# Cross-attention scores as one plain fp32 product instead of split fp32r products, an earlier closing order and all copies of turned probabilities on ScalarE, in a one-core decoder layer

## What is computed

```
x = layernorm(x + self_attention(x))                  # 32 heads of 16, alibi bias, causal
x = layernorm(x + cross_attention(x, ctx, ctx, mask)) # 32 query heads, 8 key/value heads, d 128, rope
x = layernorm(x + ffn(x))                             # relu^2 MLP 512-1024-512 + routed latent part, layernorm
```

## Time and profile before

| | |
|---|---|
| median of 3 runs | 913.37 us (911.8 to 914.2) |
| the profiled execution | 913.87 us, its span 911.5 us |
| busy: PE, DVE (VectorE), ACT (ScalarE), POOL (GpSimd) | 869.6, 654.2, 473.1, 556.1 us |
| mean granted TensorE clock | 0.988 of full speed |

### The profile page before, as it was taken

One profiled execution on the slowest core, in us unless ns is written; L12 is line 12 of the kernel. 1 busy time (PEld: TensorE's weight loads), 2 busy tenths in 40 slices (PEclk: granted clock), 3 DMA queues, 4 the chain that ended last, 5 costly groups with the idle time before them and its releaser, 6 DMA issues.

```text
span 911.5 us, 15714 instructions
## 1 busy us (share of the span) xinstructions
PE 869.6 (95%) x4780; PEld 721.2 (79%) x4780; DVE 654.2 (72%) x2171; ACT 473.1 (52%) x1509; POOL 556.1 (61%) x486
## 2 busy tenths in 40 slices
PE   7998899899999799999999999999999998999995
PEld 6787777687777588888888888888888887787884
DVE  5465688778877677777777777777777778546546
ACT  5335777877773355555555555555555556340310
POOL 4625866776677666666666666666666688463002
PEclk9999999999999999999999999999999999999998
DMA  8678999768768011311311313113122123000000
GB/s 284 242 222 190 222 205 177 164 164 171 162 202 300 26 36 38 130 39 36 128 36 45 118 36 127 36 36 128 36 78 85 36 70 105 12 24 24 24 12 35
DMA packets 68370, 96.64 MB, mean 106 GB/s; under 512 B 7232, under 2 KB 44352, under 8 KB 67264
## 3 DMA queue, kind: packets, MB, share of 16 engines
q1 hardware_dynamic: 68288, 95.65, 37.4%
HBM read 68.33 MB, written 27.26 MB: 105 GB/s over the span
## 4 chain that ended last, share of the span: by engine, by line
PE 79%; POOL 6%; DVE 5%; issue 4%; ACT 3%; DMA 1%; SPq 1%; POOLq 0%; ACTq 0%; DVEq 0%
PE banks L35 65%; PE banks L1135 4%; PE banks L1115 3%; PE banks L767 3%; PE banks L785 2%; PE banks L1136 2%; PE banks L758 1%; POOL x L1683 1%; POOL B_wv L171 1%; ACT C_prob L1056 1%; DMA heads_k<-heads_k_d 1%; POOL C_t L1271 1%; POOL B_prob L581 1%; PE banks L122 1%; SPq L213 1%
## 5 line engine op out<-in xcount | busy, mean ns | idle before, releaser
L35 PE MATMUL banks<-C_wo,C_o 128*128 128x512 f32 x768 | 191.8, 399 | 1.9 <-DVE C_o L1232 1.0
L35 PE MATMUL banks<-xT,C_w 128*128 128x512 f32 x768 | 186.6, 392 | 1.1 <-DVE xT L137 0.8
L35 PEld LDWEIGHTS banks<-xT,C_w 128*128 128x128 f32 x768 | 144.3, 189 | 31.9 <-issue 2.0
L35 PEld LDWEIGHTS banks<-C_wo,C_o 128*128 128x128 f32 x768 | 140.5, 190 | 30.6 <-issue 1.9
L1047 ACT ACTIVATE C_q<-C_t 128x512 fp32r<-128x512 f32 x64 | 40.5, 632 | 166.1 <-POOL C_t L1271 166.1
L688 ACT ACTIVATE B_prob<-B_prob,B_top 128x128 f32<-128x128 f32 x256 | 99.5, 391 | 40.1 <-DVE B_top L853 40.0
L1279 POOL TENSOR_TENSOR C_q<-C_t,C_q 128x512 fp32r<-128x512 f32 x64 | 82.8, 1294 | 46.0 <-ACT C_q L1047 46.0
L1056 ACT ACTIVATE C_prob<-C_prob,C_top 128x128 f32<-128x128 f32 x256 | 99.0, 391 | 0.0
L581 POOL TENSOR_TENSOR B_prob<-B_prob,B_rden 128x512 f32<-128x512 f32 x64 | 66.5, 1041 | 36.3 <-DVE B_rden L862 36.2
L1271 POOL TENSOR_TENSOR C_t<-C_t,C_t 128x512 f32<-128x512 f32 x64 | 82.8, 1294 | 6.2 <-DVE C_t L1189 5.9
L171 POOL TENSOR_TENSOR C_w<-stage,C_w 128x512 fp32r<-128x512 f32 x32 | 41.1, 1285 | 54.6 <-ACT C_w L166 54.5
(11 more groups left out here) (147 smaller groups left out, 1918.4 us busy)
## 6 DMA issues: line engine op xcount, KB each, us to landing
C_kv<-cross_kv_d SPq DMA_DIRECT2D x8, 2048.0 KB, 8.5
cross_kv_d<-B_k_out SPq DMA_DIRECT2D x16, 512.0 KB, 3.4
cross_kv_d<-B_v_out SPq DMA_DIRECT2D x16, 512.0 KB, 4.7
stage<-wq_dram SPq DMA_DIRECT2D x32, 256.0 KB, 2.6
stage<-wo_dram SPq DMA_DIRECT2D x32, 256.0 KB, 2.6
heads_q<-heads_q_d SPq DMA_DIRECT2D x96, 64.0 KB, 4.0
heads_k<-heads_k_d SPq DMA_DIRECT2D x96, 64.0 KB, 4.1
heads_q_d<-cT SPq DMA_DIRECT2D x8, 512.0 KB, 2.6
```

Of the source, the lines that this page charges most:

```text
L35: mm = eng.matmul(out, stationary[i], moving[j], start=first and n == 0, stop=last and n == len(PASSES) - 1)
```

## The change

- Cross scores: queries and keys are no longer split. `scores` is one plain fp32 matmul of 128 columns per head, into one bank per step, the two banks in turn; it waits for `minima(n-2)`. `key_hi`, `key_lo`, `tile_hi`, `tile_lo` and the subtraction at L1202 are gone; the GpSimd sums write keys and queries directly; the mask is negated once by ScalarE and read in the per-head minimum. A stored group of keys and values is 3/4 of the size.
- Self-attention: ScalarE copies all turned probabilities, VectorE none. `add_row`, `root` and `normalise` stand one step earlier (lags 15, 16, 17); `turn` stays at 19. The first four value weight pieces are split before step 0.
- End of stage A: context pieces are loaded and split earlier (split at tiles 16, 17, 18, 18, 19, 19, 20, 20 instead of 16 to 23).

```
-KV = 4 * NT
+KV = 3 * NT
...
+    LOAD_BEHIND = {7: (0,), 9: (1,), 11: (2,), 13: (3, 4), 15: (5, 6, 7)}
+    CONTEXT_AT = (16, 17, 18, 18, 19, 19, 20, 20)
...
-            [self.CONTEXT + i - self.QK] * (i >= self.QK)
+            [self.CONTEXT + k for k, tile in enumerate(self.CONTEXT_AT) if tile == i]
...
-            if i >= self.QK // 2 and i % 2 == 1:
-                self.load_piece(eng, self.CONTEXT + (i - self.QK // 2) // 2)
-        for n in range(self.CONTEXT + C, len(self.pieces)):
-            self.load_piece(eng, n)
+            for n in self.LOAD_BEHIND.get(i, ()):
+                self.load_piece(eng, self.CONTEXT + n)
...
-    PIECES = (("k", 0, -1), ("v", 0, 0), ("v", 1, 0), ("v", 2, 1), ("v", 3, 1), ("o", 0, 3), ("o", 1, 4), ("k", 1, 6),
+    PIECES = (("k", 0, -1), ("v", 0, -1), ("v", 1, -1), ("v", 2, -1), ("v", 3, -1), ("o", 0, 3), ("o", 1, 4), ("k", 1, 6),
...
-    OT, CLOSE, ROW, ROOT, NORMAL, TURN, TAKE = 13, (14, 15), 16, 17, 18, 19, 20
+    OT, CLOSE, ROW, ROOT, NORMAL, TURN, TAKE = 13, (14, 15), 15, 16, 17, 19, 20
...
-            eng.tensor_tensor(t1, t1, t2, ALU.add).then_inc(self.s_sum, 1)
+            eng.tensor_tensor(self.k_out[j % 2][:, :, :], by_batch(t1), by_batch(t2), ALU.add).then_inc(self.s_sum, 1)
...
-        if n >= self.LT and (n - self.LT) % 2 == 0:
+        if n >= self.LT:
             self.copy_turned(eng, n - self.LT)
...
         wait(eng, self.s_pv, (m - 4) // 2 + 1)
-        eng.activation(self.pT[:, m % 4, :], self.tp, ACT.Copy).then_inc(self.s_turned[0], 1)
+        eng.activation(self.pT[:, m % 4, :], self.tp, ACT.Copy).then_inc(self.s_turned, 1)
...
-        wait(eng, self.s_turned[(m - 1) % 2], (m + 1) // 2)
+        wait(eng, self.s_turned, m)
...
-        if n >= self.LT and (n - self.LT) % 2 == 1:
-            self.copy_odd(eng, n - self.LT)
...
     def scalar_end(self, eng):
 
-        self.key_hi(eng, len(self.FILL) // 2 - 1)
         self.value_hi(eng, len(self.FILL) // 2 - 1)
-        self.copy_turned(eng, self.NS - 2)
-        eng.wait_ge(self.s_klo, len(self.FILL) // 2)
+        for m in range(self.NS - 3, self.NS):
+            self.copy_turned(eng, m)
+        eng.wait_ge(self.s_sum, len(self.FILL) // 2)
...
+    def negate_mask(self, eng):
+
+        eng.wait_ge(self.s_mask, 16)
+        eng.activation(self.mask[:, :, :], self.mask[:, :, :], ACT.Copy, scale=-1.0).then_inc(self.s_negated, 1)
...
-            wait(eng, self.s_top, n)
+            wait(eng, self.s_top, n - 1)
             tok = slice(s % 4 * S, (s % 4 + 1) * S)
-            both = self.kv[g % 2][:, 2 * S * s:2 * S * (s + 1)]
+            keys = self.kv[g % 2][:, S * s:S * (s + 1)].bitcast(F32)
             for h in range(self.Q):
-                out = self.sc[:, h // 2, h % 2, :, :].rearrange("p j s -> p (j s)")
-                q = self.q[s // 4]
-                eng.matmul(out, q[0][:, h, tok], both, start=True, stop=False)
-                mm = eng.matmul(out[:, 0:S], q[1][:, h, tok], both[:, 0:S], start=False, stop=True)
+                mm = eng.matmul(self.sc[n % 2][:, h * S:(h + 1) * S], self.q[s // 4][:, h, tok], keys, start=True, stop=True)
...
-            for a in range(2):
-                added = eng.tensor_tensor(heads[:, a], self.sc[:, a, :, 1, :],
-                                          self.mask[:, n % B, :].unsqueeze(1).broadcast_to([P, 2, S]), ALU.subtract)
-            added.then_inc(self.s_masked, 1)
-            eng.wait_ge(self.s_masked, n + 1)
             eng.memset(self.carrier[:, :], 0.0)
             for h in range(self.Q):
                 last = eng.tensor_tensor_reduce(
-                    self.prob[:, n % 2, h * S:(h + 1) * S], self.sc[:, h // 2, h % 2, 0, :],
-                    self.prob[:, n % 2, h * S:(h + 1) * S], 1.0, 3.4e38, ALU.add, ALU.min,
-                    self.top[:, n % 2, h:h + 1])
+                    self.prob[:, n % 2, h * S:(h + 1) * S], self.sc[n % 2][:, h * S:(h + 1) * S],
+                    self.mask[:, n % B, :], 1.0, 3.4e38, ALU.add, ALU.min, self.top[:, n % 2, h:h + 1])
...
-        eng.tensor_tensor(t1, t1, t2, ALU.add).then_inc(self.s_sum, 1)
+        eng.tensor_tensor(self.query(r), by_batch(t1), by_batch(t2), ALU.add).then_inc(self.s_sum, 1)
```

More of the change, by code:

```diff
@@ L473, in __init__ @@
         self.v_out = pool("v_out", 88, [P, 2, HG, 2, P], F32R)
-        self.k_out = [pool(f"k_out{i}", (96, 132)[i], [P, 4, 2, S], F32R) for i in range(2)]
+        self.k_out = [pool(f"k_out{i}", (96, 132)[i], [P, 4, S]) for i in range(2)]
         self.bout = pool("bout", 126, [P, D])
@@ L622, in gpsimd_end @@
         self.rows.root(eng, B - 2)
-        self.key_lo(eng, len(self.FILL) // 2 - 1)
         for i in (3, 4):
@@ L693, in scalar @@
             self.value_hi(eng, j)
-        j = self.tile("k", n, 2)
-        if j is not None:
-            self.key_hi(eng, j)
         self.scalar_pieces(eng, n)
@@ L712, in scalar_end @@
             self.cross.piece_hi(eng, i)
-        self.cross.tile_hi(eng, 0)
         self.cross.piece_hi(eng, 7)
-        self.cross.tile_hi(eng, 1)
         self.rows.hi(eng, B - 1)
-        for r in (2, 3):
-            self.cross.tile_hi(eng, r)
     def project(self, eng, f, part):
@@ L773, in weigh @@
         b, c = k // C, k % C
-        for odd in range(2):
-            eng.wait_ge(self.s_turned[odd], k + 1)
+        eng.wait_ge(self.s_turned, 2 * k + 2)
         if k == 0:
@@ L910, in vector @@
             eng.wait_ge(self.s_pj, self.FILL.index(("k", j)) + 1)
-            wait(eng, self.s_klo, j - 1)
+            wait(eng, self.s_sum, j - 1)
             if j == 1:
@@ L968, in __init__ @@
         self.kv = [pool(f"kv{i}", (36, 16)[i], [P, KV], F32R) for i in range(2)]
-        self.q = [[pool(f"q{half}{lo}", 72 + 16 * half + 8 * lo, [P, self.Q, HALF], F32R) for lo in range(2)]
-                  for half in range(2)]
+        self.q = [pool(f"q{half}", 72 + 8 * half, [P, self.Q, HALF]) for half in range(2)]
         self.prob = pool("prob", 132, [P, 2, D])
@@ L992, in live, with query @@
         return 0 <= n - lag < self.NS
-    def query(self, r, lo):
-        return by_batch(self.q[r // self.Q % 2][lo][:, r % self.Q, :])
+    def query(self, r):
+        return by_batch(self.q[r // self.Q % 2][:, r % self.Q, :])
     def split(self, n):
@@ L1039, in piece_hi @@
         self.ring.hi(eng, self.first + i, self.target(i)[0])
-    def tile_hi(self, eng, r):
-        eng.wait_ge(self.s_sum, r + 1)
-        if r == self.Q:
-            for i in range(2):
-                eng.wait_ge(self.before.s_vout[i], 16 * B)
-        eng.activation(self.query(r, 0), by_batch(self.t1[:, r % 2, :]), ACT.Copy).then_inc(self.s_qhi, 1)
+    def negate_mask(self, eng):
+        eng.wait_ge(self.s_mask, 16)
+        eng.activation(self.mask[:, :, :], self.mask[:, :, :], ACT.Copy, scale=-1.0).then_inc(self.s_negated, 1)
     def exponentials(self, eng, n):
@@ L1068, in scalar @@
             self.next_piece_hi(eng, 1)
-        elif n + self.PRE < self.TILES:
-            self.tile_hi(eng, n + self.PRE)
         if self.live(n, 2):
@@ L1074, in scalar @@
             eng.activation(self.o[0][:, :], self.ov, ACT.Copy).then_inc(self.s_ohi, 1)
-        if n == 2:
-            self.tile_hi(eng, n + self.PRE)
+        if n == 0:
+            self.negate_mask(eng)
         if n != 1:
@@ L1185, in rotate @@
         eng.wait_ge(self.s_pj, r + 1)
-        wait(eng, self.s_qlo, r - 1)
+        wait(eng, self.s_sum, r - 1)
         eng.tensor_tensor(by_batch(t1), by_batch(bank), cos, ALU.mult).then_inc(self.s_cos, 1)
@@ L1370, in sync @@
             if n == self.DOWN:
-                eng.wait_ge(self.before.s_qlo, self.before.TILES)
+                eng.wait_ge(self.before.s_sum, self.before.TILES)
                 for t, name in ((self.gate, "gate"), (self.gamma, "gamma"), (self.beta, "beta")):
```

61 lines of the change are left out of this document (14 added, 47 removed).

## The result

| | before | after |
|---|---|---|
| median | 913.8 us (4 runs, 911.8 to 915.9) | 891.5 us (890.6, 892.4, 890.6) |
| the profiled execution, its span | 913.87, 911.5 us | 890.58, 888.6 us |
| mean granted TensorE clock | 0.988 | 0.995 |

The ratio is 0.975, 95% interval 0.972 to 0.978. A fourth execution of the changed kernel took 1744.7 us, for a reason that no trace shows, and is left out. Forecast was 891.0.

A forecast was written before the change was run, and what follows sets the result against it. PE bounds the long stretch of stage C; elsewhere waits set the time. From 913.87 us, terms of 0, -6, -7, -7 and -2.5 gave 891.4, forecast as 891; own range 884 to 898, widened to 883 to 903 for 8 in 10.

The forecast's parts named there:

- term 3: Steps 8 to 63 of stage B: waits before turns go, value projections come slightly later; -7 us, bounds -4 and -9.
- term 2: Stage A to step 8 of stage B: earlier loads and splits shorten idles and raise the clock; -6 us, bounds 3 and 8.
- terms 2 and 5: Start of stage B, -6 us from earlier loads and splits; last steps of C, -2.5 us from dropping L1202.
- Term 1: PE's cross scores: eight plain fp32 records cost the same 0.96 us a step as eight fp32r matmuls; 0 us.
- four passes against three: Cross scores: plain fp32 time scales with passes, +0.32 us a step, +20.5 in all, 911.5 us; chance 0.06.
- a load that isn't hidden: Cross scores: each plain fp32 record pays weight load plus stream, +0.88 us a step, 947 us; chance 0.05.
- these can now start when step 3's scores are done: Early stage B: SP's 12 head-data issues start earlier, against the 2.03 us hole for head data at 98.72.
- there is cover: Stage B: ScalarE's extra copies stay hidden, 2.5 us of ScalarE per step against 2.8 of PE.
- Term 4: From stage B to stage C: three idles shrink and the clock rises; -7 us, bounds 4 and 9.
- so the whole 0.75 is gained: Last steps of C: PE's own 5.2 us a step bounds next, so removing L1202 gains 0.75 us each time.
- The third rival: Stage B: ScalarE becomes the bound, copies late by 0.15 to 0.3 us in 56 steps; 898 to 906 us; chance 0.11.
- the fourth: Starts of B and C keep their holes as other waits take over, giving 5 instead of 13; 899 us; chance 0.13.

The follow-up runs named there:

- the doubled scores: The kernel before and the changed kernel, each with every cross score computed twice; 969.0 and 950.2 us.
- `piece_loads_late`: Changed kernel with SP loading each weight piece of stage B one step later; 889.2 us, ratio to before 0.973.
- `close_late`: Changed kernel with add_row, root and normalise back at lags 16, 17, 18; 891.5 us, ratio to before 0.978.
- `four_edits`: Changed kernel with later B piece loads, odd copies on VectorE, GpSimd's normalisation before its split early in C, ScalarE's D splits after its turned copy; 884.3 us.
- `gpsimd_relieved`: Changed kernel with four normalisations in the last steps of C moved from GpSimd to VectorE; span 890.7 us.
- `exps_ahead`: Changed kernel with ScalarE's exponentials ahead of its copy of the outputs in the last three steps of C; span 892.4 us.
- `both_relieved`: Changed kernel with, in C's last steps, ScalarE's exponentials ahead of its output copy and four normalisations moved from GpSimd to VectorE; span 893.5 us.

## Why the prediction was right

The forecast of 891.0 met 891.5. That it came out to half a microsecond is luck. By the borders that the prediction draws, the terms measured -1.3, -6.1, -6.1, -8.7 and -0.6 us against 0, -6, -7, -7 and -2.5, and the misses cancel. The second and third look better so than their reasons were: the moved hole at step 12 lies in the stretch of term 3 but comes from the reason given in term 2. Below I count it there, with the border at step 13, and then two terms that gave less than predicted (2 and 5) are made up by three that gave more. The five terms' bounds, simply added, would give 881 to 904 us; the range of 884 to 898 is narrower, and the prediction does not say how it was drawn from them.

- **Term 1 (0, measured -1.3).** Right, by the reason given. A record of 128 fp32 columns at full width costs 0.112 us, an fp32r matmul of the old scores 0.115, both about the pitch of weight loads. The distance to the outputs fell from 0.96 to 0.81 us, but the group before it grew by 0.08. The check named in the forecast, that distance alone, would have shown 0.15 us a step where 0.02 were gained. The rivals of four passes against three (+0.32 us a step) and of a load that isn't hidden (+0.88) are excluded by the doubled scores. The Trainium skill (FP8 and Floating Point Precision, TensorE Precision Notes) has four passes for fp32; no run here counts passes, and read as time against three fp32r products it would be wrong for this shape.
- **Term 2 (-6, measured -3.6).** Mis-sized. By step 8, where the term ended, the lead was 6.1 us (scores of step 8 at 92.61, near the 94 of the forecast) and by step 11 7.6. The step that failed is "these can now start when step 3's scores are done": true for the heads of step 8, but it did not ask what SP is late with next. That is one weight load waiting 3.0 us for GpSimd, ahead of the heads of step 12; hole and slow clock behind it took 4.0 us back, 2.5 and 1.5. `piece_loads_late` shows this by removing it.
- **Term 3 (-7, measured -8.7).** Size nearly right, attribution partly wrong. The turns lose their waits: the six steps that hold them are 8.8 us shorter, counted at 8.4. But the earlier lags add at most 0.6 us to this (`close_late`); what goes away on GpSimd and VectorE is enough for it, by the estimate above `key_lo` alone. The sum read `normalise` as 1.25 us long and did not ask why; it takes 0.52 where GpSimd has no 128x512 operation beside it. The price of ScalarE's extra copies, for which "there is cover", is 1.9 us, at the output projections; without it the term would have been -10.6. The lateness of `value_lo`, counted at 1.4 us, did not show.
- **Term 4 (-7, measured -8.7).** Within its bounds. Holes of 0.94, 2.65 and 2.32 us became one of 2.10, and the clock went from 0.94 to 1.00. Before the change the 53 us from 272 on had about twice the time at the lower level (0.94 over 53 us) that cost 1.3 us in three executions with the changed kernel's instructions (as 0.89 and 0.90 over 16 us, see the end). So an estimated 2.5 of the 8.7 us belong to the clock, and by those three the changed kernel's profiled execution was lucky not to pay 1.3 of them.
- **Term 5 (-2.5, measured -0.6).** Mis-sized. The step that failed is "so the whole 0.75 is gained": it took PE's own work as the next bound. ScalarE's loop from its turned copy through values, exponentials and weight splits to the next turned copy was nearly as long as the chain with L1202, so the steps went from 6.88 and 6.04 us to 6.86 and 5.92. `four_edits` shortened that loop and got 1.1 us before GpSimd's steps bound.

The third rival, ScalarE as the bound of stage B, is true at a small scale (waits of 0.27 and 0.36 us, and 0.3 us at each output projection); the fourth was too pessimistic for C and half right for B.

What stays open: the transposes ahead of the scores take 0.43 us now and 0.35 before. The starts of the four follow each other at 0.108 us in both kernels, and the difference is the last step, from the fourth to the first score: 0.03 us where the score is an fp32r matmul, 0.11 where it is a plain fp32 record. Why it is so no run shows. Open is also how much of the 18 us around the scores each of the removed pieces gave.

## What to carry to other kernels

- Price a precision change first by what the splits cost the helper engines where PE waits for them: here 1.3 us came from the matmuls and some 18, by subtraction, from the work and waits of the other engines that went away with the split.
- When a wait in an in-order DMA queue is removed, look for the next entry that waits ahead of something urgent; here the hole moved by four steps and kept its size (2.03 and 2.18 us).
- Near the end of a pipeline, the gain from taking work off a chain is its distance to the second-longest loop. Write out each engine's loop per step before claiming the whole.

## What the hardware did that I had not expected

The fall of the clock behind a hole is not fixed by the instructions. The changed kernel, `gpsimd_relieved`, `exps_ahead` and `both_relieved` have the same instructions in the first 700 us, and all have the hole of 2.10 us near 295 us. The windows 289 to 297 and 297 to 305 us have granted clocks of 1.00 and 1.00 in the first, 0.89 and 0.90, 0.98 and 0.81, 0.91 and 0.87 in the others, which lost 1.3 us each there. It is the same at step 12 of B. Behind holes of some 2.2 us the changed kernel, `exps_ahead` and `both_relieved` take 4.4 us from step 12 to 13, and `gpsimd_relieved`, with the clock at 1.00, takes 2.9. Behind the hole of 1.25 us near 805 us the clock stays at 1.00 in the changed kernel and falls to 0.79 in `gpsimd_relieved`. Runs of one kernel that differ by 1.8 us, as 890.6 and 892.4, would fit one such stretch more or less, which the profiles don't cover. It is why differences under 2 us between single executions were read only inside a stretch. In the 415 us in which PE of the changed kernel had no idle time the granted clock is 1.00.

The second thing is the length of `normalise` on VectorE (L114, 128x512). In the kernel before, GpSimd's L581, an operation of the same size, runs beside it at five of the six turns, and it takes 1.25 us each time; in `close_late` only GpSimd's 128x1 root runs beside it at five turns, and it takes 0.52. Of the 1.1 us that a turn lost before the change, 0.7 were this. The prediction took the 1.25 us as given.
